# Expert results added into the output tensor itself, with padding lanes sent to rows of other tiles

## What is computed

```python
x = x + gnn(layernorm(x), edges, ...)          # "x1" below
xf = layernorm(x)
probs = softmax(xf @ Wg + bg)                  # 8 experts
mask = (the two largest probs of the node)
for e in range(8):
    h = gelu(xf @ W1[e] + b1[e])               # 512 -> 256
    y = h @ W2[e] + b2[e]                      # 256 -> 512
    out = out + (probs * mask)[:, e:e + 1] * y
return x + out
```

## Time and profile before

| | |
|---|---|
| median of three executions | 826.9 us |
| the profiled execution, its device time | 827.44 us |
| its span (first to last instruction) | 825.8 us |
| TensorE matmul busy, share of the span | 669.4 us, 81% |
| VectorE | 441.2 us, 53% |
| ScalarE | 398.1 us, 48% |
| GpSimd | 466.7 us, 57% |
| L571, adds `result<-y,si` | 44, mean 1.601 us of GpSimd each |
| L562, gathers `xg<-xn_table,gi` | 44, mean 1.052 us of GpSimd each |
| `out_dram<-result`, two DMAs of 2500 KB | 16.8 and 18.3 us from issue to landing |

### The profile page before, as it was taken

One profiled execution on the slowest core, in us unless ns is written; L12 is line 12 of the kernel. 1 busy time (PEld: TensorE's weight loads), 2 busy tenths in 40 slices (PEclk: granted clock), 3 DMA queues, 4 the chain that ended last, 5 costly groups with the idle time before them and its releaser, 6 DMA issues.

```text
span 825.8 us, 14415 instructions
## 1 busy us (share of the span) xinstructions
PE 669.4 (81%) x3136; PEld 515.0 (62%) x3137; DVE 441.2 (53%) x1126; ACT 398.1 (48%) x1085; POOL 466.7 (57%) x531
## 2 busy tenths in 40 slices
PE   3989568988888888898899998496169999999960
PEld 3767447777766677777777776253057777777730
DVE  5999535665566556665666665871962222222210
ACT  4333255655555555555666664475004444444430
POOL 6000277777777777777777773110054777777750
PEclk9999879999999999999999999698569999999995
DMA  6242377777777777777777774499623677777767
GB/s 206 103 144 106 96 214 210 213 194 195 193 193 193 198 208 208 210 201 210 208 208 211 210 212 122 145 371 358 248 78 67 122 129 125 126 133 127 133 78 253
DMA packets 58539, 147.75 MB, mean 179 GB/s; under 512 B 8916, under 2 KB 18756, under 8 KB 58120
## 3 DMA queue, kind: packets, MB, share of 16 engines
q0 software_dynamic: 35456, 107.63, 53.1%
q1 hardware_dynamic: 22968, 37.16, 13.0%
q10 hardware_dynamic: 80, 2.56, 1.0%
HBM read 118.97 MB, written 33.47 MB: 185 GB/s over the span
## 4 chain that ended last, share of the span: by engine, by line
POOL 37%; PE 29%; issue 15%; DVE 9%; DMA 3%; SPq 2%; ACT 1%; POOLq 0%; DVEq 0%; ACTq 0%
POOL rows L479 37%; PE ps L792 9%; PE ps L802 9%; PE ps L628 4%; PE ps L784 2%; PE ps L674 1%; PE ps L777 1%; DMA x_all<-in_x_dram 1%; DMA xn_table<-xn 1%; DVE junk L1055 1%; PE ps L724 1%; DVE rows L1051 1%; DVE acc L1237 1%; SPq L432 1%; DVE hot_r L1346 1%
## 5 line engine op out<-in xcount | busy, mean ns | idle before, releaser
L479 POOL DMA_INDIRECT rows<-node_table,srcT x316 | 312.4, 989 | 179.0 <-issue 96.0
L674 PE MATMUL ps<-rows,S 128*128 128x257 f32 x1568 | 359.3, 386 | 64.0 <-DVE S L1136 61.7
L674 PEld LDWEIGHTS ps<-rows,S 128*128 128x128 f32 x1568 | 294.4, 191 | 128.7 <-DVE S L1136 78.0
L874 ACT ACTIVATE E<-sdst_b,rows 128x128 f32 x784 | 237.4, 388 | 177.4 <-DMA rows<-node_table,srcT 177.3
L1130 DVE SCALAR_TENSOR_TENSOR Wt<-E 128x512 f32<-128x512 f32 x98 | 68.0, 694 | 119.7 <-ACT E L874 106.8
L1136 DVE SCALAR_TENSOR_TENSOR S<-node_id,dstT,Wt 128x128 f32<-128x128 f32 x392 | 111.9, 347 | 23.9 <-DVE Wt L1130 23.9
L1143 DVE TENSOR_TENSOR acc<-acc,ps 128x514 f32 x99 | 67.9, 686 | 35.0 <-PE ps L674 27.1
L792 PE MATMUL ps<-W_e,xgT 128*128 x352 | 84.8, 385 | 0.0
L802 PE MATMUL ps<-W_e,hidT 128*128 x176 | 82.8, 593 | 0.6 <-ACT hidT L971 0.6
L571 POOL DMA_INDIRECT result<-y,si x44 | 70.5, 1601 | 17.8 <-POOL gi L519 11.5
L792 PEld LDWEIGHTS ps<-W_e,xgT 128*128 128x128 f32 x352 | 64.6, 194 | 7.2
(11 more groups left out here) (191 smaller groups left out, 468.3 us busy)
## 6 DMA issues: line engine op xcount, KB each, us to landing
W_e<-in_L_ffn_W_dram SPq DMA_DIRECT2D x16, 512.0 KB, 6.1
node_table<-rows SPq DMA_DIRECT2D x20, 258.0 KB, 2.7
result<-acc SPq DMA_DIRECT2D x20, 256.0 KB, 4.8
xn_table<-xn SPq DMA_DIRECT2D x20, 256.0 KB, 5.3
rows<-node_table,srcT POOLq DMA_INDIRECT x316, 3.8
x_all<-in_x_dram SPq DMA_DIRECT2D x19, 256.0 KB, 3.2
out_dram<-result SPq DMA_DIRECT2D x1, 2500.0 KB, 16.8
out_dram<-result ACTq DMA_DIRECT2D x1, 2500.0 KB, 18.3
```

The costliest lines, as they stand in the source:

```text
L479: nc.gpsimd.indirect_dma_start(out=rows[:, g % RING, c, :], out_offset=None, in_=table, in_offset=bass.IndirectOffsetOnAxis(ap=srcT[:, GC ...
L674: m = pe.matmul(ps_agg[q][:, a, 0:HALF], S[:, w, c, :], rows[:, r, c, a * HALF:(a + 1) * HALF], start=(c == 0), stop=(c == GC - 1))
L874: m = nc.scalar.activation(e[:, q, c, :], sdst_b[:, bass.ds(tile * P, P)], ACT.Exp, bias=bias, scale=scale)
```

## The change

`result` is gone. x1 is stored to `out` directly, the last tile by GpSimd in four pieces of 17 rows, one for each add slot. The adds go into `out`, and SyncE only waits for them at the end. The padding lanes now add their zeros to rows of `out`: in the last tile of an expert the k-th padding lane gets the k-th node, among the first 128, that has not its place in this very tile; a tile behind the last in use gets rows 0 to 127. These nodes may stand in other tiles of the expert. So `need` also counts, as a point from which all adds ahead must have landed, the last tile of each expert and the first three tiles behind the last in use (19 points instead of 8). The rows of the padding lanes are computed by VectorE and TensorE inside the first steps of the expert stage, and the table `need` is moved there too.

```diff
             for u in range(NX, NT // 2):
-                x_step(u, u % 2)
+                x_step(u, u % 2, u == NT // 2 - 1)
...
-            sp.dma_start(out[0:N // 2, :], result[0:N // 2, :]).then_inc(st_out, 16)
-            sp.wait_ge(st_out, 32)
+            sp.sem_inc(all_out, 1)
+            sp.wait_ge(all_out, 1)
...
                         pool.wait_ge(put_y[(r + 1 - LAG) % YR], slot_count(i + 1 - LAG, r + 1 - LAG))
+                    if peeled and i + 1 == LAG:
+                        pool.wait_ge(dst_ok, 1)
                     copy_si(i + 1 - LAG, (r + 1 - LAG) % YR)
...
                     nc.gpsimd.indirect_dma_start(
-                        out=result, out_offset=bass.IndirectOffsetOnAxis(ap=si[:, (r - LAG) % YR, :], axis=0),
+                        out=out, out_offset=bass.IndirectOffsetOnAxis(ap=si[:, (r - LAG) % YR, :], axis=0),
...
             pool.wait_ge(x1_ok, NT)
+            each = -(-LAST // YR)
             for r in range(YR):
-                nc.gpsimd.dma_start(halves(result[NTN + r * P:NTN + (r + 1) * P, :]), features(NT - 1))\
-                    .then_inc(put_y[r], 16)
+                first_row, end_row = min(r * each, LAST), min((r + 1) * each, LAST)
+                nc.gpsimd.dma_start(halves(out[(NT - 1) * P + first_row:(NT - 1) * P + end_row, :]),
+                                    acc[first_row:end_row, NT - 1, :, 0:HD]).then_inc(put_y[r], 16)
...
                 new, mid, old = parts
+                if peeled and new and 2 <= n <= 3:
+                    pad_products(n - 1)
...
+            def pad_products(k):
+
+                pe.wait_ge(pad_ok, k)
+                if k == 1:
+                    m = pe.matmul(ps_pad[:, 0:NX], below[:, :], pad_n[:, 3, :], start=True, stop=True)
+                else:
+                    for e in range(NX + 1):
+                        m = pe.matmul(ps_dst[:, 0:4 * ROUNDS], hot_pad[:, e, :], pad_v[:, e, :],
+                                      start=(e == 0), stop=(e == NX))
+                m.then_inc(pad_ps, 1)
...
-            for r in range(YR):
-                act.wait_ge(put_y[r], 16 * n_rounds + 16)
-            act.dma_start(out[N // 2:N, :], result[N // 2:N, :]).then_inc(st_out, 16)
-            act.wait_ge(st_out, 32)
...
-            link(V.tensor_single_scalar(inv[:, 1, :], inv[:, 2, :], 0.0, ALU.is_lt))
-            link(V.tensor_tensor(inv[:, 1, :], inv[:, 1, :], beyond[:, 0:TILES], ALU.mult))
-            link(V.tensor_tensor(dst_row[:, 0:TILES], inv[:, 0, :], inv[:, 1, :], ALU.add))
             V.memset(spare[:, 0:1], 0.0).then_inc(routed, 1)
             hot_share(1)
             hot_share(2)
...
+            def needs():
+                link(V.tensor_copy(points[:, 0:NX], per[0:1, 5, :]))
+                link(V.tensor_single_scalar(points[:, NX:2 * NX], per[0:1, 3, :], -1.0, ALU.add))
+                link(V.tensor_scalar(points[:, 2 * NX:], count[0:1, 0:3], per[0:1, 3, NX - 1:NX], None, ALU.add))
+                every = points[:, :].unsqueeze(1).to_broadcast([1, n_tiles, 2 * NX + 3])
...
+            def rows_of_pads():
+
+                dve.wait_ge(pad_ps, 2)
+                link(V.tensor_scalar(pad_to[:, :], ps_dst[:, 0:n_tiles], -1.0, 0.0, ALU.add, ALU.max))
+                V.tensor_copy(dst_row[:, TILES:n_tiles], pad_to[:, TILES:])
+                V.tensor_tensor(dst_row[:, 0:TILES], inv[:, 0, :], pad_to[:, 0:TILES], ALU.add).then_inc(dst_ok, 1)
...
+                if peeled and new and 1 <= n <= 4:
+                    (pads_in_last_tile, pads_by_lane, rows_of_pads, needs)[n - 1]()
                 if old:
                     e = expert_in(dve, e_old)
```

More of the change, by code:

```diff
@@ L172, in gnn_moe_kernel @@
         si = sg("si", [P, YR, 1], I32)
+        total = sg("total", [P, NX], F32)
         b1_b = sg("b1_b", [P, NX, F], F32)
@@ L183, in gnn_moe_kernel @@
         part1 = sg("part1", [P, 1], F32)
-        beyond = sg("beyond", [P, 4 * ROUNDS], F32)
-        beyond_i = sg("beyond_i", [P, 4 * ROUNDS], I32)
+        pad_n = sg("pad_n", [P, 6, NX], F32)
+        pad_to = sg("pad_to", [P, 4 * ROUNDS], F32)
+        hot_pad = sg("hot_pad", [P, NX + 1, P], BF16)
+        pad_v = sg("pad_v", [P, NX + 1, 4 * ROUNDS], BF16)
         valid = sg("valid", [P, 2, NT], F32)
@@ L426, in load_W2, with x_step @@
                              .rearrange("p e k d -> p (e k) d")).then_inc(ld_W2, 16)
-            def x_step(u, s):
+            def x_step(u, s, last=False):
                 sp.wait_ge(x1_ok, 2 * u + 2)
                 for j in range(2):
-                    sp.dma_start(halves(result[bass.ds((2 * u + j) * P, P), :]), features(2 * u + j)).then_inc(st_x1, 16)
+                    if not (last and j == 1):
+                        rows_of = out[0:(NT - 1) * P, :].rearrange("(t p) d -> t p d", p=P)[bass.ds(2 * u + j, 1)]
+                        sp.dma_start(halves(rows_of.rearrange("t p d -> (t p) d")), features(2 * u + j))\
+                            .then_inc(st_x1, 16)
                 store_xn(u, s)
@@ L1400, in _ @@
-            link(V.tensor_single_scalar(adds_i[:, :, :], adds_i[:, :, :], 2, ALU.arith_shift_right))
-            link(V.tensor_tensor(adds_f[:, :, :], adds_i[:, :, :],
-                                 place_i[:, :].unsqueeze(1).to_broadcast([1, n_tiles, YR]), ALU.mult))
-            link(V.tensor_reduce(first_tile[:, :], adds_f[:, :, :], AX.X, ALU.add))
-            V.tensor_copy(need[:, :], first_tile[:, :]).then_inc(need_ok, 1)
             dve.wait_ge(inv_ps, 2)
             V.tensor_copy(share[:, 0:TILES], ps_share[:, 0:TILES]).then_inc(share_ok, 1)
+            n_tiles = 4 * ROUNDS
@@ new lines, in _, with pads_in_last_tile @@
+            place, chosen, from_, in_last, lane, last_tile_of = (pad_n[:, k, :] for k in range(6))
+            def pads_in_last_tile():
+                link(V.tensor_tensor(place, rank[:, :, 0], rank[:, :, NT], ALU.add))
+                link(V.tensor_tensor(chosen, choice[:, :, 0, 0], choice[:, :, 1, 0], ALU.add))
+                link(V.tensor_single_scalar(last_tile_of, per[:, 3, :], -1.0, ALU.add))
+                link(V.tensor_single_scalar(from_, last_tile_of, float(P), ALU.mult))
+                link(V.tensor_tensor(in_last, place, from_, ALU.is_ge))
+                V.tensor_tensor(in_last, in_last, chosen, ALU.mult).then_inc(pad_ok, 1)
@@ new lines, in pads_by_lane @@
+            def pads_by_lane():
+                link(V.scalar_tensor_tensor(out=lane, in0=per[:, 2, :], scalar=-float(P), in1=total[:, :],
+                                            op0=ALU.mult, op1=ALU.add))
+                link(V.tensor_scalar(lane, lane, part1[:, :], float(P - 1), ALU.add, ALU.add))
+                dve.wait_ge(pad_ok, 1)
+                link(V.scalar_tensor_tensor(out=lane, in0=in_last, scalar=float(4 * P), in1=lane,
+                                            op0=ALU.mult, op1=ALU.add))
+                dve.wait_ge(pad_ps, 1)
+                link(V.tensor_tensor(lane, lane, ps_pad[:, 0:NX], ALU.subtract))
+                V.tensor_tensor(hot_pad[:, 0:NX, :], lane.unsqueeze(2).to_broadcast([P, NX, P]),
+                                count_b[:, :].unsqueeze(1).to_broadcast([P, NX, P]), ALU.is_equal)
+                V.tensor_copy(hot_pad[:, NX, :], ident[:, :])
+                link(V.tensor_tensor(pad_v[:, 0:NX, :], last_tile_of.unsqueeze(2).to_broadcast([P, NX, n_tiles]),
+                                     count_b[:, 0:n_tiles].unsqueeze(1).to_broadcast([P, NX, n_tiles]), ALU.is_equal))
+                link(V.tensor_scalar(pad_v[:, NX, :], count_b[:, 0:n_tiles], per[:, 3, NX - 1:NX], None, ALU.is_ge))
+                V.tensor_scalar(pad_v[:, :, :], pad_v[:, :, :], part1[:, :], None, ALU.mult).then_inc(pad_ok, 1)
```

37 lines of the change are left out of this document (20 added, 17 removed).

## The result

The changed kernel takes 838.45 us (median of four, 835.49 to 843.34), the kernel before 828.01 us beside it (818.91 to 829.84). The ratio is 1.0161, with a 95% interval of 1.0104 to 1.0218: slower, and clear of noise. By that ratio the change costs 13 us (9 to 18), while the medians are 10.4 us apart.

The account below looks back on a forecast made before the run. TensorE bounds the expert stage, the copy the end; GpSimd's waits would take over. Add 3 at 652.1, plus 176.5 and 5.5, gives 834.1; with 1.5 clock, 1.6 around, 0.5 less: 837 us, 8 in 10 from 824 to 848.

Parts of the forecast that it names:

- The copy: End of the kernel: without copying `result` to `out` it would end at about 807.2, 18.6 us earlier.
- The end of the routing: Three small VectorE operations in front of `routed` go away; the first gather comes 0.7 us earlier.
- Two waits for each expert: GpSimd in the expert stage: 16 waited steps instead of 7, 6.25 us each; add 3 to add 43 takes 176.5 us.
- The start: First expert tiles: padding rows and a late `need` make tile 6 9.3 us late; add 3 at 652.1.
- The clock: TensorE around tile 6, after lying nearly idle: two steps at the lower clock level, 1.5 us added.
- The sum: Whole kernel: span ends at 834.1 instead of 825.8, plus 1.5 for clock and 1.6 around the span; 837 us.
- Waits that are cheap or hidden: Two rivals, expert stage: waits cheap or start half as late, 824 to 831 us, chance 0.17; waits hidden, 809 to 818, 0.04.
- A hidden start: Rival, start of expert stage: the gather of tile 6 is not held up by `need`; 825 us, chance 0.05.
- A clock that falls again and again: Rival, expert stage: each pair of waits idles TensorE and lowers its clock; from 844 us, chance 0.17.
- The signs: Profile after: gather 6 19 us later, first add 13, GpSimd's `gi` waits 30 us or more, TensorE 90% busy.
- The landing: Adds in the expert stage land 5.0 us after start by trace; the skill's 2.6 us would make waits cost nothing.

Follow-up runs that it names:

- e1: The kernel before without the two closing copies, so the output is not written; 808.05 us, ratio 0.9764.
- e4: The kernel before with only the changed kernel's 19 wait points, made at the old place; padding rows and copy as before; 844.16 us, ratio 1.0176.
- e8: e4 with a third wait for each expert, at its second tile; measured once, 863.76 us.
- e7: e4 with the second wait of each expert moved from its last tile to its third; measured once, 850.37 us.
- e2: The changed kernel with its table `need` made ahead of the expert stage, padding rows still in the first steps; 832.96 us, ratio 1.0094.
- e3: The kernel before with its own 8-point table of waits made late, in the step of tile 4; 830.38 us, ratio 1.0049.
- e5: The changed kernel with padding lanes sent to fixed rows of an expert's first two tiles, and an early 16-point table; 817.49 us, ratio 0.9861.
- e6: e5 with GpSimd waiting for the landing of its last adds before its closing step; 810.89 us, ratio 0.9857.

## Why the forecast held, step by step

- **The copy.** The step that sized it said that the kernel would end at the landing, 18.6 us earlier. It was 15.4 in the traces (24.3 to 8.9), 14.7 in e1. The step was wrong in its last part: it took SyncE's wait as the end and did not see GpSimd's DRAIN, which had no row in the groups because the copy covered it. Yet it could be read in the trace of the kernel before: the DRAIN from 801.3 to 811.4, 4.4 us behind the copies' start at 807.00, speaks for an end about 14 us earlier and not 18.6.
- **The end of the routing.** 0.7 us expected, 0.7 found.
- **Two waits for each expert.** 176.5 us from add 3 to add 43 forecast, 176.6 measured, 177.5 in e4 where nothing else was changed. The price of a waited step, taken as the mean of seven, and 3.36 for the others were enough (6.25 for each, 6.23 found); e8 shows that the sum also holds with 23 waits (198 and 199.5). The text made something of it that the two stand in a row; e7 shows that waits apart do not help, and cost 6.60 each. What the text said of the mechanism, that late gathers starve TensorE, covers 10.5 of the 16.7 us. The other 6.2 are the waits before adds 42 and 43, behind which no gather stands: the sum had them, the text did not say that they are paid whatever TensorE does.
- **The start.** I forecast T(3), the transposes of tile 3, 15.4 us behind tile 0; it was 16.5. Gather 6: 29.6 forecast (640.6 against tile 0 at 611.0), 30.5 found. Add 3: 41.1 and 42.2. The waits of TensorE for VectorE were 1.73 and 1.78 us, forecast 1 and 2. The missing 1.1 us are the lower clock during the W1 product of tile 1 (0.57 granted, 3.21 us instead of 1.89).
- **The clock.** I added 1.5 us for the lower level behind tile 6. The transposes of tile 6 did take 1.12 us, but adds 0 to 3 came in 10.1 us as in the sum without it, so at that place it cost nothing; it cost about as much one step earlier.
- **The sum.** From tile 0 on: forecast 834.1 + 1.5 - 611.0 = 224.6 us, found 227.7. The 3.1 between them are the DRAIN (8.9 instead of 5.5 behind the last add, 3.4), 1.1 at the start, less the 1.5 for the clock. Against the kernel before the trace lost 13.6 us from tile 0 on where the sum said 10.5. The median came out at 838.45 against 837, the difference of the medians at +10.4 against +10.1. That is closer than the parts, and so luck: the end of the graph layer alone differs by 16.6 us between the ten traces (509.3 to 525.9), and the ratio puts the loss at 13 us.
- **The rivals.** Waits that are cheap or hidden: e4 excludes them. A hidden start: e2 and e3 exclude it. A clock that falls again and again: 1.00 in the stage here.
- **The signs.** The gather of tile 6 came 22.9 us later than 621.60 and the first add 16.8 us later than 629.18 (forecast 19 and 13), of which 2.3 lie ahead of tile 0. GpSimd waited for landings 24.3 us in 10 places for `gi`, less than the 30 that I named; with the 11.2 in 3 for `si` it is 35.5 in 13. TensorE waited for gathers in 10 places and 12.3 us, where I had forecast once for each expert and 15 us or more; it was busy 94% of the stage, not 90%. And what ends last is not an add but GpSimd's DRAIN.
- **The landing.** By the Trainium skill (DMA: Bandwidth & Descriptors, Anatomy of one DMA) these adds would take 2.6 us, an estimate from its 2.0 us and 436 GB/s. That does not fit in the changed kernel either: they land in 4.5 to 5.3 us.

## What to carry to other kernels

A copy at the end of a kernel can be cheaper than the ordering that its absence asks for. Ask first what a new wait does to the engine that issues in order: here a waited step costs 6.2 us against 3.36, and with two for each expert an engine that was busy 114 of the stage's 162 us becomes the bound, because the next gathers stand behind the wait. A wait before the very last adds is paid in full, as nothing runs beside it (6 us here). If adds must be kept apart, choose the rows so that the order already given keeps them apart (e5), and make tables while the engine that makes them has nothing else to do. And subtract from the cost of any last stage what runs beneath it.

## What I had not expected of the hardware

GpSimd's closing DRAIN ends 3.9 to 4.4 us behind the landing of its last DMA, by the time at which SyncE knows of it. It lasted 8.9 to 10.1 us where it began with the last add, and still 5.2 us where everything had landed before (e6). What it does in that time stays open. The time to the first tile of the expert stage differed by 15 us (605.3 to 620.6) between kernels with no edit ahead of it, which is more than the effect of this change; only times measured from that tile show it. Even these differ by up to 2.5 us at add 3 from trace to trace (29.1 to 31.6); from add 3 to add 43 the four traces with the waits of before and an early table agree within 0.1 us.
